# A gated two-layer Flamingo block on one Trainium2 core: the three-product form of P times V for the last three pairs of heads of attention 0, in place of the last eight

## The reference, cut to what matters

```python
def _heads(x):                                   # (b, s, 512) -> (b, 16, s, 32)
    b, s, _ = x.shape
    return x.reshape(b, s, H, W).transpose(0, 2, 1, 3)
q, k, v = _heads(x_q @ Wq.T + bq), _heads(x_k @ Wk.T + bk), _heads(x_v @ Wv.T + bv)
scores = jnp.einsum('bhqw,bhkw->bhqk', q, k) / np.sqrt(W)
scores = scores - 10000.0 * (1.0 - m)            # mask, in layer 0 only
p = jax.nn.softmax(scores, axis=-1)
h = jnp.einsum('bhqk,bhkw->bhqw', p, v)          # P times V
...
x = x + tanh(g_xattn[0]) * attention0(layernorm(x), ctx, ctx, mask)
x = x + tanh(g_ffn[0])   * ffn0(layernorm(x))    # silu(x w1) * (x w2), gelu(h1), gelu(h2), w3
x = x + tanh(g_xattn[1]) * attention1(layernorm(x), ctx, ctx)   # with an output projection
x = x + tanh(g_ffn[1])   * ffn1(layernorm(x))    # quantized gate, up and down
```

## Time and profile before

| | |
|---|---|
| time, median of 3 runs | 1575.21 us (1574.67 to 1576.0) |
| span of the profiled execution | 1573.8 us; the page gives no other time for it |
| PE busy | 1562.0 us (99%) |
| DVE busy | 1025.1 us (65%) |
| ACT busy | 972.5 us (62%) |
| POOL busy | 426.0 us (27%) |
| granted TensorE clock | 1.000, mean of the core |
| last pairs of attention 0 | 457 to 485 us of the span |

### The profile page before, as it was taken

One profiled execution on the slowest core, in us unless ns is written; L12 is line 12 of the kernel. 1 busy time (PEld: TensorE's weight loads), 2 busy tenths in 40 slices (PEclk: granted clock), 3 DMA queues, 4 the chain that ended last, 5 costly groups with the idle time before them and its releaser, 6 DMA issues.

```text
span 1573.8 us, 25733 instructions
## 1 busy us (share of the span) xinstructions
PE 1562.0 (99%) x9306; PEld 1428.1 (91%) x9306; DVE 1025.1 (65%) x1814; ACT 972.5 (62%) x2014; POOL 426.0 (27%) x570
## 2 busy tenths in 40 slices
PE   9999999999999999999999999999999999999999
PEld 7999899999989999999999998889999989988765
DVE  6577887787786562123644425637777777778987
ACT  5676777677775455444544435447677767767676
POOL 4221222222145222222322222311211121123741
PEclk9999999999999999999999999999999999999999
DMA  8766767687582225554365642576676677658500
GB/s 246 190 169 167 200 179 198 160 206 182 137 220 98 95 81 201 185 180 165 106 230 192 214 165 93 179 181 184 160 193 175 169 189 179 171 142 225 193 13 31
DMA packets 149974, 261.29 MB, mean 166 GB/s; under 512 B 41136, under 2 KB 94000, under 8 KB 149709
## 3 DMA queue, kind: packets, MB, share of 16 engines
q1 hardware_dynamic: 149505, 259.24, 58.8%
q10 hardware_dynamic: 332, 0.23, 0.1%
HBM read 191.01 MB, written 58.57 MB: 159 GB/s over the span
## 4 chain that ended last, share of the span: by engine, by line
PE 94%; DVE 3%; ACT 2%; issue 1%; DMA 0%; ACTq 0%; DVEq 0%
PE ps L1237 33%; PE ps L864 16%; PE ps L868 14%; PE ps L964 8%; PE ps L942 8%; PE ps L1171 2%; PE ps L1033 2%; PE ps L884 2%; PE ps L931 2%; PE ps L926 2%; PE ps L1188 1%; PE ps L929 1%; PE ps L930 1%; ACT P L1955 1%; PE ps L1082 1%
## 5 line engine op out<-in xcount | busy, mean ns | idle before, releaser
L1237 PE MATMUL ps<-ah_f,wh_f 128*128 128x400 f32 x1288 | 442.0, 344 | 0.0
L1237 PE MATMUL ps<-al_f,wh_f 128*128 128x400 f32 x1288 | 441.3, 343 | 0.0
L2319 POOL TENSOR_TENSOR cxl<-raw,cxh 128x384 fp32r<-128x384 f32 (+1 forms) x112 | 105.7, 965 | 556.9 <-ACT cxh L1897 556.9
L1819 DVE TENSOR_TENSOR wl_f<-raw_f,wh_f 128x1024 fp32r<-128x1024 f32 x85 | 103.7, 1223 | 232.2 <-POOL wh_f L2309 232.2
L1386 DVE TENSOR_REDUCE nmax<-ps 100x1 f32<-100x722 f32 x256 | 220.8, 903 | 33.2 <-PE ps L930 29.6
L1237 PEld LDWEIGHTS ps<-al_f,wh_f 128*128 128x128 f32 x1288 | 242.2, 188 | 0.0
L1237 PEld LDWEIGHTS ps<-ah_f,wh_f 128*128 128x128 f32 x1288 | 241.9, 188 | 0.1
L1955 ACT ACTIVATE P<-ps,nmax 100x722 f32<-100x722 f32 x256 | 220.4, 864 | 27.4 <-DVE nmax L1386 27.2
L1967 ACT ACTIVATE PT<-ps 128x400 fp32r<-128x400 f32 x384 | 165.9, 505 | 70.3 <-PE ps L942 69.2
L2237 ACT ACTIVATE raw_f<-wl_f 128x1024 f32<-128x1024 f32 x88 | 93.4, 1062 | 173.7 <-DVE wl_f L1819 173.6
L1392 DVE TENSOR_TENSOR PT<-ps,PT 128x400 fp32r<-128x400 f32 x384 | 196.3, 566 | 3.2
(11 more groups left out here) (227 smaller groups left out, 2669.0 us busy)
## 6 DMA issues: line engine op xcount, KB each, us to landing
KS<-kd SPq DMA_DIRECT2D x192, 361.0 KB
raw_f<-in_h SPq DMA_DIRECT2D x64, 512.0 KB, 4.2
raw_f<-in_gud SPq DMA_DIRECT2D x48, 512.0 KB, 4.3
raw<-in_ctx SPq DMA_DIRECT2D x64, 192.0 KB, 3.5
raw_f<-in_w SPq DMA_DIRECT2D x24, 512.0 KB, 3.5
kd<-ksh SPq DMA_DIRECT2D x60, 192.0 KB, 2.2
kd<-ksl SPq DMA_DIRECT2D x60, 192.0 KB, 2.5
raw<-in_ctx SPq DMA_DIRECT2D x64, 169.0 KB, 4.4
```

Source lines behind the costliest of these rows:

```text
L1237: return e.matmul(o, p, q, start=start, stop=stop)
L1819: e.tensor_tensor(wl[:, z, :], raw[:, r, :], raw32(wh[:, z, :]), ALU.subtract).then_inc(v_ul, 1)
L2319: e.tensor_tensor(m.cx[1][:, k, off:off + n], m.raw[:, k, off:off + n], raw32(m.cx[0][:, k, off:off + n]), ALU.subtract).then_inc(g_cx, 1)
```

## The change

One number in `summed` changes. The three-product form of P times V is used for the pairs 61 to 63 of attention 0, where it was used for 56 to 63; the pairs 56 to 60 take the usual form.

```diff
 def summed(L, i):
 
-    return L == 0 and i >= NP - 8
+    return L == 0 and i >= NP - 3
```

## The result

| | before | changed |
|---|---|---|
| time, median of 5 | 1574.89 us (1574.67 to 1576.0) | 1582.07 us (1580.82 to 1582.57) |
| span of the profiled execution | 1573.8 us | 1580.1 us |
| mean granted TensorE clock | 1.000 | 0.996 |

The change makes the kernel slower by 0.42%; the ratio of the times is 1.0042, with an interval of 1.0031 to 1.0053. The forecast was 1581.2 us in a range of 1577.8 to 1583.5. In a second series of five the changed kernel took 1581.1 us beside 1575.46, the median of sixteen executions of the kernel before; two more of its executions, at 2579.7 us with a granted clock of 0.557 and at 3131.7 us, were in a slow state and are left out.

A forecast was written before the change was run, and what follows sets the result against it. The last pairs of attention 0 were taken as bound by ACT's exps, with DVE nearly abreast, not by PE. Terms 1.08 + 0.83 + 1.75 + 1.67 + 0.15 + 0.5 = 5.98 us gave 1581.2 us, range 1577.8 to 1583.5.

The forecast's parts named there:

- What bounds the last pairs: Last pairs of attention 0: PE waits for ACT's exps, so the 3.8 us saved on PE count for nothing.
- The chain of 3.10 us from the copy to the exp: Iterations 58 to 61: ACT's copy, three DVE additions, both maxima, then the exp take 3.10 us, read at iteration 52.
- Iterations 58 to 61: Time to the copy's place on ACT plus 3.10 us lengthens these iterations by 1.08, 0.83, 1.75 and 1.67 us.
- Iteration 62: Additions for pair 60 hold no maxima up; ACT's longer copy adds 0 to 0.2 us, taken as 0.15.
- The end: Iteration 62 to L973: DVE's statistics start 0.70 us later; PE has 0.16 us to spare, so +0.5 us.
- The clock rival: PE, less busy in iterations 60 and 61, loses the full clock: 4 to 7 us over the forecast, 1587; chance 0.06.
- The added DVE work as the whole cost: Rival for the last pairs: copy at hand when DVE arrives, only its added work counts; 1.4 us, 1576.6; chance 0.08.
- Nothing is given back behind L973: From L973 on PE runs the FFN without a pause and shifts as a whole, so the added 5.98 us stay.
- Span and time: Profiled span 1573.8 us, median of the runs 1575.21, 1.4 us above it; the 5.98 us are added to the median.

The follow-up runs named there:

- The experiments with the order on DVE and on ACT: Changed kernel, additions behind DVE's maxima: 1578.8 us, iteration 60 too: 1577.14; changed kernel, ACT's copy ahead of the extras in iterations 59 to 61: 1579.55.
- Pair 60 alone: Kernel before with the usual form for pair 60 only, three-product form for the others of the last eight; 1575.96 us, ratio 1.0003.
- the maxima first: Changed kernel with DVE's additions behind the two maxima in iterations 58 to 61, iteration 60 included; 1577.14 us, ratio 1.001.
- with the pauses partly filled: Changed kernel with the six matmuls of P and V done twice for pairs 56 to 60; 1580.84 us, ratio 1.0038.
- with 18 matmuls a pair: Kernel before, with DVE's copy also waiting for ACT's copy of the same pair, for pairs 56 to 60; 1578.58 us, ratio 1.0019.

## Why the prediction was right, point by point

- *What bounds the last pairs.* Right. The 3.8 us taken off PE gave nothing back: in no kernel with the usual form is any distance shorter than before by over 0.03 us.
- *The chain of 3.10 us from the copy to the exp*. Right, and it carried the forecast. In the changed kernel: 461.81 - 458.71 = 3.10, 466.74 - 463.63 = 3.11, 472.56 - 469.47 = 3.09, 478.55 - 475.45 = 3.10.
- *Iterations 58 to 61:* forecast +1.08, +0.83, +1.75, +1.67, measured +1.07, +0.83, +1.74, +1.66. The experiments with the order on DVE and on ACT show that the place of the additions and of the copy is the cause.
- *Iteration 62:* forecast +0.15, measured +1.28. This step was mis-sized. Pair 60 alone shows 0 for its own part, and the changed kernel at full clock there has the 4.10 us of before; the 1.28 are the lower clock, under which PE's last scores, transposes and matmuls doubled (12 transposes 2.21 us, 1.19 at full clock) and PT came late.
- *The end:* forecast +0.5, measured +0.70; 0.52 without the clock (pair 60 alone).
- *The clock rival* had 0.06. The fall itself came in every profiled execution of the changed kernel, so as a forecast of the clock that chance was far too low. By the sign that the prediction gives for it (a clock below 1.00 in iterations 60 and 61) this rival came true beside the forecast. I had argued from the length of PE's single pauses, put at 2 to 3 us; they were at most 1.60 us and the clock fell all the same. PE's share in iteration 60 was put at 51%; at full clock the second profile has 4.29 of 5.83 us there, 74%, and the first 3.26 of 4.93 us, 66%, in iteration 59. Its price was put too high, 4 to 7 us: both times it was back at 1.00 before the FFN, and much of it fell in time in which PE would have waited (iteration 60 took 5.82 us with it and 5.83 without). That left 0.2 to 1.5 us.
- *The added DVE work as the whole cost* was put at 1.4 us. It didn't decide the change, but with the maxima first it is what remains: 1.58 us by the trace, 1.8 by the median.
- *Nothing is given back behind L973.* Right: +7.28 less 0.82 of head start is 6.46, and the spans differ by 6.3.
- *Span and time:* I put 1.4 us around the span by taking the median. The profiled execution of the changed kernel took 1582.07 with a span of 1580.1, so it is 2.0; the forecast doesn't hang on it, as it adds to the median.

Part of the closeness is luck: the changed kernel's ten runs lie between 1580.78 and 1582.57, the kernel's before also move by over a microsecond, and the clock's share of 0.2 to 1.5 us wasn't in the sum, which stood 0.16 us above what the trace shows at full clock (5.82).

## What to carry to other kernels

Before work is moved off the engine that the page shows as 94% of the chain, look for who is last in the stretch itself; there the saved 3.8 us were worth nothing. A change of form often changes who waits for whom: find the sequence elsewhere in the same trace, measure it from start to start (3.10 us here), and set it at the place in the waiting engine's written order, together with all that stands ahead of it there. That gave four terms to within 0.01 us, and it foretold the nearly double price of two pairs, which have unrelated work (L2237, four L1988) ahead of them in ACT's queue.

## What the runs showed of the hardware that I had not expected

TensorE's granted clock fell to the lower level though no pause of PE was longer than 1.60 us. Nor was a long pause needed: in the changed kernel's second profile it fell at 459.5, and PE's longest pause in the iteration before that was 0.56 us. The windows there, in the same columns as above:

```profile
458.00:459.00 1.00, 0.44 (x2) 1.00 1.00 256
459.00:460.00 1.00, 0.63 (x4) 0.74 1.08 397
460.00:461.00 1.00, 1.00 (x6) 0.50 1.05 422
```

The same instructions stand one microsecond earlier in the first profile, with the same 0.44 and 0.63 us of work, and there the clock stayed at 1.00:

```profile
457.00:458.00 1.00, 0.44 (x2) 1.00 1.01 256
458.00:459.00 1.00, 0.63 (x4) 1.00 1.09 400
459.00:460.00 1.00, 1.00 (x14) 1.00 1.03 414
```

So the same program with the same work just before keeps the clock in one execution and loses it in another, and neither one pause nor the last two microseconds settle where it falls. How much PE does over the iterations does matter: with the pauses partly filled (5.10 us busy of 5.82) the clock was 1.00 in five executions of five, and with 18 matmuls a pair (4.90 of 5.31) in eleven of eleven, where the changed kernel had 0.996 to 0.998 in ten of ten. With the maxima first in iteration 60 too, the usual form kept 1.00 in ten executions of eleven, with PE busy 3.05 of 4.17 us in iteration 60. What exactly decides isn't shown. The Trainium skill ("TensorE: Matmul & The Clock Gate", the section on a second failure mode by cycling PSUM queues) tells of short idle times of PE between groups of matmuls, frequent enough to make the clock go down and up again; these traces agree in that the clock fell and came back twice in each profile of the changed kernel, with no pause above 1.60 us. Where it falls differs from one execution to the next, and so does its price: 0.2 us in one profile and about 1.5 in the other, for the same program.
